# Router, scan and expert tiles on one NeuronCore: transposes of the norms moved by half a tile, combines split, a scatter put ahead of a gather

## What is computed

```python
def ffn(x):                      # 8 routed experts, top 2, and 2 shared ones, inner width 640
    scores = sigmoid(x @ w_router.T)
    topk_w, topk_i = top_k(scores, 2); topk_w /= topk_w.sum()
    out = sum over the 2 chosen experts e of topk_w * ((silu(x @ wg[e].T) * (x @ wu[e].T)) @ wd[e].T)
    return out + the same with sg, su, sd for both shared experts

def scan(x):                     # 16 states for each of 256 channels
    proj = x @ W_xproj.T; dt = softplus(proj[:, :256]); B, C = the two times 16 columns after it
    h = exp(dt * A) * h + dt * B * x     # along the 256 positions, for each state
    return (h * C).sum(states) + D * x

x = x + 0.5 * ffn(layernorm(x))
x = x + scan(layernorm(x))
x = x + 0.5 * ffn(layernorm(x))
```

## Time and profile before

| | us |
|---|---|
| median of 3 runs | 561.29 |
| lowest and highest | 558.7 and 562.9 |
| profiled execution, its own time | 560.26 |
| its span | 558.3 |
| PE busy in the span | 522.4 |
| DVE busy in the span | 327.4 |
| POOL busy in the span | 231.5 |

### The profile page before, as it was taken

One profiled execution on the slowest core, in us unless ns is written; L12 is line 12 of the kernel. 1 busy time (PEld: TensorE's weight loads), 2 busy tenths in 40 slices (PEclk: granted clock), 3 DMA queues, 4 the chain that ended last, 5 costly groups with the idle time before them and its releaser, 6 DMA issues. The chain is left out here.

```text
span 558.3 us, 11040 instructions
## 1 busy us (share of the span) xinstructions
PE 522.4 (94%) x4356; PEld 423.1 (76%) x4357; DVE 327.4 (59%) x654; ACT 157.6 (28%) x336; POOL 231.5 (41%) x208
## 2 busy tenths in 40 slices
PE   2999999999978999999998899999999989999995
PEld 2998998448937999546896799884478989954695
DVE  3553335512546999995596699999656522222224
ACT  1111122222117444451311844444221111222210
POOL 1022000220415999992354499999302520000041
PEclk9999999999978999999999999999989999999999
DMA  7999788210305456531221456454101320110021
GB/s 230 398 407 353 275 305 290 69 67 22 95 14 136 119 124 150 148 91 31 93 86 50 126 125 120 134 148 111 30 11 51 105 75 29 39 39 12 19 60 65
DMA packets 41988, 67.70 MB, mean 121 GB/s; under 512 B 5040, under 2 KB 24752, under 8 KB 41936
## 3 DMA queue, kind: packets, MB, share of 16 engines
q1 hardware_dynamic: 31344, 44.69, 27.6%
q10 hardware_dynamic: 7024, 12.19, 6.0%
q0 software_dynamic: 3568, 10.10, 5.4%
HBM read 48.74 MB, written 18.22 MB: 120 GB/s over the span
## 5 line engine op out<-in xcount | busy, mean ns | idle before, releaser
L492 PEld LDWEIGHTS ps<-xt,w_gu 128*128 128x128 f32 x1360 | 161.1, 197 | 11.7 <-ACT xt L746 8.2
L492 PE MATMUL ps<-xt,w_gu 128*128 128x128 f32 x1360 | 165.1, 282 | 4.7 <-ACT xt L746 4.2
L965 DVE SCALAR_TENSOR_TENSOR hb<-hb,ps 128x640 f32<-128x640 f32 x68 | 55.5, 817 | 152.2 <-ACT hb L728 152.0
L517 PE MATMUL ps<-w_dn,hb 128*128 128x256 f32 x520 | 120.7, 379 | 0.0
L517 PEld LDWEIGHTS ps<-w_dn,hb 128*128 128x128 f32 x520 | 94.9, 190 | 10.8
L728 ACT ACTIVATE hb<-ps 128x640 f32<-128x640 f32 x68 | 47.4, 697 | 160.9 <-PE ps L492 148.2
L911 POOL DMA_INDIRECT region<-yg_rows,ypos x32 | 31.0, 968 | 146.0 <-DMA yg_rows<-ob 128.7
L492 PEld LDWEIGHTS ps<-xnt,w_gu 128*128 128x128 f32 x720 | 85.9, 197 | 1.6 <-issue 0.8
L492 PE MATMUL ps<-xnt,w_gu 128*128 128x128 f32 x720 | 86.7, 281 | 0.0
L943 POOL TENSOR_TENSOR xnt<-xnt,hh 128x512 f32<-128x512 f32 x64 | 81.5, 1277 | 0.0
L1010 DVE TENSOR_TENSOR_SCAN ps<-ps,region 128x512 f32<-128x512 f32 x64 | 78.2, 1222 | 0.3 <-POOL region L930 0.2
(11 more groups left out here) (102 smaller groups left out, 321.8 us busy)
## 6 DMA issues: line engine op xcount, KB each, us to landing
bcb<-bc_rows SPq DMA_DIRECT2D x22, 512.0 KB, 5.1
region<-bc_rows SPq DMA_DIRECT2D x10, 512.0 KB, 4.8
xg<-xg_rows SPq DMA_DIRECT2D x34, 128.0 KB
w_gu<-in_wg SPq DMA_DIRECT2D x4, 640.0 KB, 13.2
w_gu<-in_wu SPq DMA_DIRECT2D x4, 640.0 KB, 14.4
w_dn<-in_wd SPq DMA_DIRECT2D x4, 640.0 KB, 16.8
w_gu<-in_wg ACTq DMA_DIRECT2D x4, 640.0 KB, 4.7
w_gu<-in_wu ACTq DMA_DIRECT2D x4, 640.0 KB, 5.7
```

Of the source, the lines that this page charges most:

```text
L492: last = nc.tensor.matmul(gup(p)[:, c * P:(c + 1) * P], w_gu4[:, e, k, c * P:(c + 1) * P], x, start=(k == 0), stop=(k == KC - 1))
L517: ins = nc.tensor.matmul(outp(p), hb[:, p, c * P:(c + 1) * P], w_dn4[:, e, c, :], start=(c == 0), stop=(c == IC - 1))
L965: nc.vector.scalar_tensor_tensor(out=h, in0=h, scalar=1.0, in1=gup(p)[:, 0:I], op0=ALU.add, op1=ALU.mult).then_inc(s_a, 1)
```

## The change

The list and some waits are changed; no instruction of arithmetic is added or taken away.

1. In segment 3 one more shared tile stands ahead of the routed ones, so that the first routed tile is 56 and the last 64 (before 55 and 63), and three shared tiles follow them (before four).
2. T of each norm but the first two stands behind `first` of a tile (gate and up of the next) and ahead of its `second`: the down projection comes between T and what uses `xnt` (X1 or R1). The scans begin one tile later and still have 11 tiles.
3. In the scan's first tile all three half states stand behind the body. The scaling of `xnt` by D on ACT (L852) is part of the third of them, and POOL waits for it one step later.
4. Combine 0 is split in two around the tile S1-1, combine 1's first half moves ahead of R2 and S of segment 2, combine 3 is split around the eviction of tile 66, and combine 2 stands after tile S3+1, two tiles further on.
5. R2 and S of segments 2 and 3 stand one tile further on. For segment 3, O 2 and G 2 come behind S 3 and one more tile; before, they stood ahead of R2 3 and S 3. S 3 no longer waits for the gathers.
6. The overflow steps take the number of the tile ahead of them from a function.

```diff
@@
-          SHARED[0] + ROUTED + SHARED[1]]
+          SHARED[0] + SHARED[1][:1] + ROUTED + SHARED[1][1:]]
@@ def half_states(first, n, part):
     a = PER_TILE * (n - first)
-    a, b = (a, a + 2) if part == 0 else (a + 2, a + PER_TILE)
+    early = 0 if n == first else 2
+    a, b = (a, a + early) if part == 0 else (a + early, a + PER_TILE)
     return range(min(a, HALVES), min(b, HALVES))
@@ SCHEDULE
-    ("tiles", S1 + 14, S1 + 15), ("R2", 2), ("S", 2), ("tiles", S1 + 15, S2 - 1), ("C", 1, 0, 2),
-    ("tiles", S2 - 1, S2), ("C", 1, 2, TT), ("N", "A", 1), ("tiles", S2, S2 + 1), ("T", "A", 1), ("X1", 1),
+    ("tiles", S1 + 15, S1 + 16), ("C", 1, 0, 2), ("R2", 2), ("S", 2),
+    ("tiles", S2 - 1, S2), ("C", 1, 2, TT), ("N", "A", 1), ("tiles", S2, S2 + 1),
+    ("first", S2 + 1), ("T", "A", 1), ("second", S2 + 1), ("X1", 1),
...
-    ("tiles", S2 + 14, S2 + 15), ("O", 2), ("G", 2), ("R2", 3), ("S", 3), ("tiles", S2 + 15, S3), ("C", 2, 0, TT),
-    ("tiles", S3, S3 + 13), ("O", 3), ("G", 3), ("tiles", S3 + 13, TILES - 1), ("C", 3, 0, TT),
-    ("tiles", TILES - 1, TILES),
+    ("tiles", S2 + 15, S2 + 16), ("R2", 3), ("S", 3), ("tiles", S2 + 16, S3), ("O", 2), ("G", 2),
+    ("tiles", S3, S3 + 2), ("C", 2, 0, TT), ("tiles", S3 + 2, S3 + 14), ("O", 3), ("G", 3), ("tiles", S3 + 14, TILES - 2), ("first", TILES - 2),
+    ("C", 3, 0, 3), ("second", TILES - 2), ("C", 3, 3, TT), ("tiles", TILES - 1, TILES),
@@ ACT, states
                     m, d = g // KC, g % KC
+                    if g == KC:
+                        act.wait_ge(s_dtx, KC * (h + 1))
+                        for k in range(KC):
+                            ins = nc.scalar.activation(xnt[:, k, :], xnt[:, k, :], ACT.Copy, scale=dpar[:, k:k + 1])
+                        ins.then_inc(s_skip, 1)
@@ ACT, scan
                         states(start, n, 0, h)
-                        if n == start:
-                            act.wait_ge(s_dtx, KC * (h + 1))
-                            for d in range(KC):
-                                ins = nc.scalar.activation(xnt[:, d, :], xnt[:, d, :], ACT.Copy,
-                                                           scale=dpar[:, d:d + 1])
-                            ins.then_inc(s_skip, 1)
                         body(n)
@@ POOL, S
-                    if s >= 2:
+                    if s == 2:
                         for t in range(TT):
                             pool.wait_ge(s_gat[t], 2 * 16 * s)
@@ POOL, scan
-                    pool.wait_ge(s_skip, h + 1)
                     for g in range(HALVES):
                         d = g % KC
                         if g + KC < HALVES:
                             input_of(g + KC)
                         pool.wait_ge(s_hc, HALVES * h + g + 1)
+                        if g == 0:
+                            pool.wait_ge(s_skip, h + 1)
```

More of the change, by code:

```diff
@@ L129 @@
     ("tiles", 0, 6), ("N", "P", 1), ("tiles", 6, 8), ("T", "P", 1), ("tiles", 8, 9), ("R1", 1),
-    ("tiles", 9, 10), ("R2", 1), ("S", 1), ("tiles", 10, S1 - 2), ("O", 0), ("G", 0), ("tiles", S1 - 2, S1),
-    ("C", 0, 0, TT), ("N", "A", 0), ("tiles", S1, S1 + 1), ("T", "A", 0), ("X1", 0),
-    ("scan", S1 + 1, S1 + 12, 0), ("first", S1 + 12), ("Y", 0), ("N", "P", 2), ("second", S1 + 12),
-    ("tiles", S1 + 13, S1 + 14), ("T", "P", 2), ("O", 1), ("G", 1), ("R1", 2),
-    ("tiles", S1 + 14, S1 + 15), ("R2", 2), ("S", 2), ("tiles", S1 + 15, S2 - 1), ("C", 1, 0, 2),
@@ L135 @@
-    ("tiles", S2 - 1, S2), ("C", 1, 2, TT), ("N", "A", 1), ("tiles", S2, S2 + 1), ("T", "A", 1), ("X1", 1),
-    ("scan", S2 + 1, S2 + 12, 1), ("first", S2 + 12), ("Y", 1), ("N", "P", 3), ("second", S2 + 12),
-    ("tiles", S2 + 13, S2 + 14), ("T", "P", 3), ("R1", 3),
-    ("tiles", S2 + 14, S2 + 15), ("O", 2), ("G", 2), ("R2", 3), ("S", 3), ("tiles", S2 + 15, S3), ("C", 2, 0, TT),
-    ("tiles", S3, S3 + 13), ("O", 3), ("G", 3), ("tiles", S3 + 13, TILES - 1), ("C", 3, 0, TT),
-    ("tiles", TILES - 1, TILES),
-]
+    ("tiles", 9, 10), ("R2", 1), ("S", 1), ("tiles", 10, S1 - 2), ("O", 0), ("G", 0), ("tiles", S1 - 2, S1 - 1),
@@ new lines @@
+    ("C", 0, 0, 2), ("tiles", S1 - 1, S1), ("C", 0, 2, TT), ("N", "A", 0), ("tiles", S1, S1 + 1),
+    ("first", S1 + 1), ("T", "A", 0), ("second", S1 + 1), ("X1", 0),
+    ("scan", S1 + 2, S1 + 13, 0), ("first", S1 + 13), ("Y", 0), ("N", "P", 2), ("second", S1 + 13),
+    ("O", 1), ("G", 1), ("first", S1 + 14), ("T", "P", 2), ("second", S1 + 14), ("R1", 2),
+    ("tiles", S1 + 15, S1 + 16), ("C", 1, 0, 2), ("R2", 2), ("S", 2),
+    ("tiles", S2 - 1, S2), ("C", 1, 2, TT), ("N", "A", 1), ("tiles", S2, S2 + 1),
@@ new lines @@
+    ("first", S2 + 1), ("T", "A", 1), ("second", S2 + 1), ("X1", 1),
+    ("scan", S2 + 2, S2 + 13, 1), ("first", S2 + 13), ("Y", 1), ("N", "P", 3), ("second", S2 + 13),
+    ("first", S2 + 14), ("T", "P", 3), ("second", S2 + 14), ("R1", 3),
+    ("tiles", S2 + 15, S2 + 16), ("R2", 3), ("S", 3), ("tiles", S2 + 16, S3), ("O", 2), ("G", 2),
+    ("tiles", S3, S3 + 2), ("C", 2, 0, TT), ("tiles", S3 + 2, S3 + 14), ("O", 3), ("G", 3), ("tiles", S3 + 14, TILES - 2), ("first", TILES - 2),
+    ("C", 3, 0, 3), ("second", TILES - 2), ("C", 3, 3, TT), ("tiles", TILES - 1, TILES),
+]
@@ L142, with last_ahead_of_overflow @@
+def last_ahead_of_overflow(s):
+    last = None
+    for step in SCHEDULE:
+        if step[0] in ("tiles", "scan"):
+            last = step[2] - 1
+        elif step[0] == "second":
+            last = step[1]
+        elif step == ("O", s):
+            return last
 NORM = {key: k for k, key in enumerate(x[1:] for x in SCHEDULE if x[0] == "N")}
@@ L461, in _ @@
                         sp.sem_inc(s_none, 1)
-                elif kind == "C" and step[1] == 2:
+                elif kind == "C" and step[1] == 2 and step[3] == TT:
                     sp.wait_ge(s_comb, 3 * TT)
                     sp.dma_start(out[0:HALF, :].rearrange("(t p) h -> p t h", p=P), xres[:, 0:TT, :]).then_inc(s_fin, 16)
-                elif kind == "C" and step[1] == 3:
+                elif kind == "C" and step[1] == 3 and step[3] == TT:
                     sp.wait_ge(s_comb, 4 * TT)
@@ L599, in overflow @@
             def overflow(s):
-                o, n = s_o[s], last_routed(s)
+                o, n = s_o[s], last_ahead_of_overflow(s)
                 q = n % 2
@@ L774, in overflow @@
                 o = s_o[s]
-                q = last_routed(s) % 2
+                q = last_ahead_of_overflow(s) % 2
                 act.wait_ge(s_pos, s + 1)
```

## The result

| | before | changed |
|---|---|---|
| median of 4 runs each, us | 560.56 | 569.88 |
| lowest and highest, us | 558.7 and 562.9 | 568.87 and 570.7 |
| profiled execution, its own time, us | 560.26 | 569.24 |
| its span, us | 558.3 | 567.2 |

The changed kernel takes 1.0163 times as long, 95% interval 1.0118 to 1.0208: 9 us slower, which is outside the 1% that was named as the bound. 569.0 us was predicted. (Before has one execution more here than in the table ahead of the prediction.)

What follows compares the result with a forecast made beforehand. PE is nearly always at work, so its waits count, within a scan only as far as DVE gets on. 560.26 +2.4 by tile 56, +0.9 end, +4.5 clock is 568.1; median 1.0 above, said as 569.0, range 566 to 572.

Steps and rivals of the forecast that it cites:

- First scan: First scan: PE waits 1.1 us in gate and up of tile 19; hidden(21) comes at 187.9, 5.6 us earlier.
- DVE's 17.96 us: First scan: DVE's time from X1's end to hidden(20) before, taken as unchanged ahead of hidden(21).
- Second scan: Second scan: power behind scatter 2 ends at 303.2, PE waits 10.3 us for evictions; kernel then 0.7 us later than before.
- rival 2: Scatters don't hold POOL; the power and gather 2 get past them, both long waits go: 551.8 us, chance 0.1.
- Segment 3: Start of segment 3: combine 2 ends 34.6 us after R2, PE waits 6.6; tile 56 starts 2.4 us later, without clock.
- The 6.6: Segment 3, gate and up of tile 55: PE waits 6.6 us for DVE, which stands in combine 2.
- the two terms together: Segment 3: PE's wait of 6.6 us in tile 55 and 2.0 us of clock behind it.
- The end: From last routed tile to last eviction 19.3 us: +0.7 for combine 3's late last row tile, +0.2 for transposes.
- Clock: Behind the two long waits PE's clock falls, costing 2.5 us at the second scan and 2.0 in segment 3.
- Rival 1: The clock holds through both long waits, at the second scan and in segment 3: 564.5 us, chance 0.2.
- The Trainium skill's price of a gather's landing: Last gather, at the end: 2.3 us from issue of 128 KB to landing; the end some 0.6 us earlier.
- The sum: Whole kernel: +2.4 by tile 56, +0.9 at the end, +4.5 of clock, +7.8 on the profiled 560.26.

Runs made afterwards that it cites:

- experiment 7: Version 3 with combine 0 whole behind tile S1-1, as before the change: 554.12 us, ratio 0.9874 to before.
- experiment 4: The changed kernel with the first scan tile's half states two ahead of the body and one behind, as before: 567.34 us, ratio 1.0167 to before.
- experiments 1: The changed kernel with scatter 2 listed behind the norm of the second scan: 559.62 us, ratio 1.0020 to before.
- version 3: The changed kernel with scatter 2 behind the second scan's norm and combine 2 behind tile 55: 550.75 us, ratio 0.9862 to before.

## Why the prediction was right

| step | predicted | measured |
|---|---|---|
| wait ahead of the first T | 1.1 | 1.25 |
| hidden(21) | 187.9 | 188.40 |
| second scan, power ends | 303.2 | 303.96 |
| waits for evictions ahead of T | 10.3 | 9.4 (1.57 + 7.84) |
| end of X1, second scan | 319.6 with clock | 320.82 |
| clock behind the long wait | 2.5 | 3.0 |
| R2 of segment 3 to the end of combine 2 | 34.6 | 34.1 |
| R2 of segment 3, gate and up behind it | 430.3 with clock | 431.89 |
| wait in tile 55 | 6.6 | 4.58, and 0.92 in tile 54 |
| clock behind it | 2.0 | 1.6 |
| gate and up of tile 56 later by | 6.9 | 7.5 |
| last routed tile to the last eviction | 19.3 | 19.8 |

**First scan.** Right in kind. The gain was 5.1 and not 5.6 us: the eviction of tile 17 ended at 161.05 and not 160.2, since PE came to gate and up of tile 19 0.6 us late (156.12 for 155.56) and the split of combine 0, taken for 0.5, gave 0.2 (4.93 us from there to the eviction's end, 5.15 before; experiment 7 agrees). From X1's end to hidden(21) it then took 17.59 us and not 17.96. The wait for `xt` came back two tiles later than before, not one, within the rate of DVE (hidden(22) 7.51 us behind hidden(21)). I had the states' place within DVE's 17.96 us, and experiment 4 bears that out.

**Second scan.** The step that decided the sign: the scatters hold POOL (rival 2 was that they don't). The power began on the instruction at which the eighth scatter let go, and taking the scatter from in front of it gave 8.0 us, near the 6.1 + 2.5 that rival 2 put on it. The clock there was taken too small, 2.5 for a measured 3.0.

**Segment 3.** Combine 2 ended 34.1 us after R2. The wait behind it was 4.58 us in this profile, where a pause that the profile puts down to no instruction of the kernel, 0.92 us and 1.3 with the slower pieces around it, came ahead of it; in experiments 1 and 4, which have the same order there, it was 5.94 and 5.89. The 6.6 was 0.7 too long. Moving the combine gave 8.0 us, where the two terms together said 8.6.

**The end.** +0.7 and +0.2 predicted, 1.4 measured. The gather's length was right (from its first DMA to the last products 14.00 us, 548.94 to 562.94, for 14.05); it began 4.30 us behind the last routed tile and not 3.87.

**Clock.** Rival 1, that it holds through both long waits, fell: 0.50 behind both. The Trainium skill ("TensorE: Matmul & The Clock Gate", the section on HAM oscillation) tells of a kernel whose TensorE waits 3 to 5 us for a DMA between short bursts, is throttled again in each wait and starts each burst cold. For 7.84, 5.9 and 4.58 us the trace agrees. The waits of 1.57 and 1.74 us that stayed in version 3 are shorter than that page's and kept full clock (8 pieces in 1.16 us behind each). The Trainium skill's price of a gather's landing ("DMA: Bandwidth & Descriptors", anatomy of one DMA on the software path: 2.0 us and bytes over 436 GB/s, an estimate of 2.3 us) would have put the end 0.6 us earlier. Here the last gather DMA began on POOL at 560.18 and its products on DVE at 562.94, 2.8 us later; the measurement decides. The end came 0.5 us later than the sum from rows, and so 1.1 later than by that price.

**The sum.** 7.8 us were added up and 9.0 measured in the profiled executions (569.24 less 560.26). R2 of segment 3 came 1.6 us later than by the terms (0.5 of it clock, 0.5 from the first scan; R2 of segment 2 was 1.1 late already, 281.18 for 280.06, and what added 0.6 on the way there is not traced); the stretch from there to tile 56 was 0.9 shorter, with the shorter wait and clock; the end cost 0.5 more. The errors are small and partly cancel, so that it is in part luck that the sum is only 1.2 off and 569.0 still closer to the median of 569.88.
